# The eight modulation matrices as fp32 products instead of pairs of fp16 terms

## The reference

```
# layer 0                                        # layer 1
scale1 = cond @ ln1_tw.T                         ada = silu(cond) @ Wada.T + bada     # 64 x 3072
h = rms(x) * (ln1_w * (1 + scale1))              gamma1, gamma2, scale1, scale2, shift1, shift2 = split(ada, 6)
x = x + attention(rope(h @ Wq, h @ Wk), h @ Wv) @ Wo.T     x = x + attn(ln(x) * (scale1 + 1) + shift1) * gamma1
scale2 = cond @ ln2_tw.T                         x = x + (gelu((ln(x)*(scale2+1)+shift2) @ Wfc1.T + bfc1) @ Wfc2.T + bfc2) * gamma2
h = rms(x) * (ln2_w * (1 + scale2))
x = x + (silu(h @ Wg.T) * (h @ Wu.T)) @ Wd.T
```

## Time and profile before

| | us |
|---|---|
| median of 3 runs | 2768.59 (2766.93 to 2770.6) |
| the profiled execution, its own time | 2764.49 |
| its span, first to last instruction | 2762.7 |
| mean granted TensorE clock | 0.969 |
| TensorE busy (matmuls) | 2524.8 (91%) |
| VectorE busy | 1395.9 (51%) |
| ScalarE busy | 962.3 (35%) |
| GpSimd busy | 1040.4 (38%) |

### The profile page before, as it was taken

How to read it: one execution, slowest core, us unless ns; L and a number is a source line. 1 busy time by engine, 2 the same in 40 slices (tenths; PEclk the granted TensorE clock), 3 DMA queues, 4 the chain that set the end, 5 groups by cost and what they waited for, 6 DMA issues and landing times.

```text
span 2762.7 us, 47260 instructions
## 1 busy us (share of the span) xinstructions
PE 2524.8 (91%) x18552; PEld 1255.8 (45%) x18552; DVE 1395.9 (51%) x2115; ACT 962.3 (35%) x1549; POOL 1040.4 (38%) x1007
## 2 busy tenths in 40 slices
PE   2449999999999999999997769999999999999998
PEld 1224445454444444444443335454454545454543
DVE  4554434243342524435224657575767667575742
ACT  2332213132231322223122336262626354444532
POOL 1112223132231322223121546564655555565632
PEclk9669999999999999999999889999999999999999
DMA  6430010100001010010205111212121112112110
GB/s 201 132 98 3 7 45 3 50 3 28 26 5 48 3 46 7 12 40 4 76 3 179 36 43 29 74 31 76 28 66 44 55 42 60 48 45 65 32 54 27
DMA packets 115019, 129.40 MB, mean 47 GB/s; under 512 B 53758, under 2 KB 56190, under 8 KB 114820
## 3 DMA queue, kind: packets, MB, share of 16 engines
q1 hardware_dynamic: 114820, 126.36, 15.2%
HBM read 71.79 MB, written 18.87 MB: 33 GB/s over the span
## 4 chain that ended last, share of the span: by engine, by line
PE 73%; issue 10%; DVE 7%; POOL 5%; ACT 4%; DMA 0%; POOLq 0%; SPq 0%; DVEq 0%; ACTq 0%
PE ps_m L1440 38%; PE ps_abef L1440 18%; PE ps_d L1440 2%; PE ps_c L1440 2%; PE ps_abef L1619 2%; PE ps_abef L1621 2%; PE ps_abef L1626 2%; PE ps_abef L1653 1%; PE ps_d L1607 1%; POOL h_mlp L815 1%; POOL inner L837 1%; POOL scratch L868 1%; PE ps_abef L1642 1%; PE ps_abef L1661 1%; PE ps_c L1475 1%
## 5 line engine op out<-in xcount | busy, mean ns | idle before, releaser
L1440 PE MATMUL ps_m<-h_mlp,weights 128*128 128x512 f16 x3072 | 708.5, 383 | 38.9 <-POOL h_mlp L815 19.1
L1440 PE MATMUL ps_m<-weights,inner 128*128 128x512 f16 x3072 | 690.4, 379 | 8.7 <-DVE scratch L1280 8.7
L1440 PEld LDWEIGHTS ps_m<-h_mlp,weights 128*128 128x128 f16 x3072 | 296.8, 99 | 384.9 <-issue 38.4
L1440 PEld LDWEIGHTS ps_m<-weights,inner 128*128 128x128 f16 x3072 | 296.9, 98 | 346.1 <-DVE scratch L1280 6.5
L837 POOL TENSOR_TENSOR inner<-scratch,inner 128x512 f16<-128x512 f32 x256 | 301.0, 1176 | 315.6 <-ACT inner L1000 315.6
L1440 PE MATMUL ps_abef<-h_mlp,weights 128*128 128x512 f16 x1536 | 345.4, 379 | 0.0
L1440 PEld LDWEIGHTS ps_abef<-h_mlp,weights 128*128 128x128 f16 x1536 | 147.6, 98 | 173.0
L806 POOL TENSOR_TENSOR scratch<-scratch 128x1 f32<-128x1 f32 x128 | 29.1, 228 | 434.3 <-ACT scratch L945 379.1
L1000 ACT CAST inner<-scratch 128x512 f16<-128x512 f32 x256 | 156.6, 612 | 101.6 <-DVE scratch L1408 68.1
L815 POOL TENSOR_TENSOR h_mlp<-scratch,h_mlp 128x512 f16<-128x512 f32 x64 | 74.0, 1156 | 199.2 <-ACT h_mlp L958 199.2
L1278 DVE SCALAR_TENSOR_TENSOR scratch<-scratch,ps_m 128x512 f32<-128x512 f32 x64 | 44.0, 688 | 198.2 <-ACT scratch L1008 198.2
(11 more groups left out here) (169 smaller groups left out, 3646.3 us busy)
## 6 DMA issues: line engine op xcount, KB each, us to landing
x_mlp<-x_attn SPq DMA_DIRECT2D x64, 256.0 KB, 2.3
weights<-gamma SPq DMA_DIRECT2D x128, 128.0 KB, 2.9
scratch<-scratch SPq DMA_DIRECT2D x128, 128.0 KB, 2.6
x_attn<-x SPq DMA_DIRECT2D x32, 256.0 KB, 2.7
x_mid<-x_mlp SPq DMA_DIRECT2D x32, 256.0 KB, 2.0
x_attn<-x_mid SPq DMA_DIRECT2D x32, 256.0 KB, 2.7
out<-x_mlp SPq DMA_DIRECT2D x32, 256.0 KB, 2.2
inner<-wada_t SPq DMA_DIRECT2D x6, 1024.0 KB, 5.9
```

Source lines behind the costliest of these rows:

```text
L1440: ins = nc.tensor.matmul(o, left(a, k), right(b, k), start=(first and n == 0), stop=(last and n == len(order) - 1), skip_group_check=True)
```

## The change

The modulation matrices are no longer cut. TensorE multiplies them as fp32 straight from the staging buffer, with fp32 conditioning rows (`cond32` for matrices 0 and 1, `silu32` for the others). 16 fp32 matmuls of 64 columns take the place of 48 fp16 ones, and for matrices 2 and 3, whose product is stored the other way round, 4 of 512 columns the place of 12. The products wait for the load instead of the cut, and a load into a buffer that held a modulation matrix waits for that matrix's product (`s_ada`). Since these matrices don't count in `s_whi` and `s_wlo` any more, `cut_no(g)` gives the number of cut groups up to g. The factor 1/16 falls out of VectorE's modulation terms.

```
@@ load_group, on SP
-                if reuse >= 0:
-                    sp.wait_ge(s_wlo, reuse + 1)
+                if reuse >= 0 and groups[reuse][0] == "ada":
+                    sp.wait_ge(s_ada, ada_before(reuse) + 1)
+                elif reuse >= 0:
+                    sp.wait_ge(s_wlo, cut_no(reuse))
...
@@ ScalarE
-            nc.scalar.copy(cond_cut[:, 0], cond32).then_inc(s_setup_act, 1)
-            nc.scalar.activation(xn[:, 0:256].rearrange("p (k b) -> p k b", k=KC), cond32, ACT.Tanh, scale=0.5).then_inc(s_setup_act, 1)
+            nc.scalar.activation(silu32, cond32, ACT.Tanh, scale=0.5).then_inc(s_setup_act, 1)
...
-            cut_hi(0)
-            for g in range(1, FIRST):
+            for g in range(2, FIRST):
                 cut_hi(g)
...
-                if FIRST + s < SETUP:
+                if FIRST + s < SETUP and groups[FIRST + s][0] == "w":
                     cut_hi(FIRST + s)
...
@@ VectorE
-            link(nc.vector.tensor_tensor(cond_cut[:, 1], cond32, cond_cut[:, 0], ALU.subtract))
-            link(nc.vector.scalar_tensor_tensor(half_silu, half_silu, 1.0, cond32, ALU.add, ALU.mult))
-            link(nc.vector.tensor_scalar(half_silu, half_silu, 0.5, None, ALU.mult))
-            link(nc.vector.tensor_copy(silu_cut[:, 0], half_silu))
-            nc.vector.tensor_tensor(silu_cut[:, 1], half_silu, silu_cut[:, 0], ALU.subtract).then_inc(s_cond, 1)
+            link(nc.vector.scalar_tensor_tensor(silu32, silu32, 1.0, cond32, ALU.add, ALU.mult))
+            nc.vector.tensor_scalar(silu32, silu32, 0.5, None, ALU.mult).then_inc(s_cond, 1)
...
-            cut_lo(0)
             dve.wait_ge(s_const, 43)
...
-                if FIRST + s < SETUP:
+                if FIRST + s < SETUP and groups[FIRST + s][0] == "w":
                     cut_lo(FIRST + s)
...
@@ TensorE
             def ada(g, n):
-                pe.wait_ge(s_wlo, g + 1)
+                landed, count, _, _ = place(g)
+                pe.wait_ge(landed, count)
                 pe.wait_ge(s_cond, 1)
...
-                c = cond_cut if n < 2 else silu_cut
+                c = cond32 if n < 2 else silu32
                 if 2 <= n < 4:
-                    ins = products([(bank[0:NSEQ, :], lambda b, k: ada_cut[:, b, k, :])],
-                                   lambda a, k: c[:, a, k, :], range(KC))
+                    for k in range(KC):
+                        ins = nc.tensor.matmul(bank[0:NSEQ, :], c[:, k, :], staged(g)[:, k, :], start=(k == 0), stop=(k == KC - 1))
                 else:
                     for f in range(KC):
-                        ins = products([(bank[:, NSEQ * f:NSEQ * (f + 1)], lambda b, k: c[:, b, k, :])],
-                                       lambda a, k: ada_cut[:, a, k, P * f:P * (f + 1)], range(KC))
+                        for k in range(KC):
+                            ins = nc.tensor.matmul(bank[:, NSEQ * f:NSEQ * (f + 1)], staged(g)[:, k, P * f:P * (f + 1)],
+                                                   c[:, k, :], start=(k == 0), stop=(k == KC - 1))
                 ins.then_inc(s_ada, 1)
```

More of the change, by code:

```diff
@@ L315, in layers_kernel @@
         cond32 = carve(256).rearrange("p (k b) -> p k b", k=KC)
-        cond_cut = carve(256).bitcast(F16).rearrange("p (h k b) -> p h k b", h=2, k=KC)
-        silu_cut = carve(256).bitcast(F16).rearrange("p (h k b) -> p h k b", h=2, k=KC)
+        silu32 = carve(256).rearrange("p (k b) -> p k b", k=KC)
         taken["scratch"] = base
@@ L527, in dest, with cut_no @@
         def dest(g, hl):
-            if groups[g][0] == "ada":
-                return ada_cut[:, hl]
             return groups[g][1][:, hl]
+        def cut_no(g):
+            return sum(1 for q in groups[:g + 1] if q[0] == "w")
         def weight_scale(g):
@@ L643, in _ @@
                 load_group(g)
-            sp.wait_ge(s_setup, 17)
+            sp.wait_ge(s_setup, 14)
             sp.dma_start(rope_dram[:, :, 0, :], cos_t.rearrange("p (t f) -> p t f", f=32)).then_inc(s_rope_st, 16)
@@ L733, in _ @@
                     store_y(L0, x_mid, NBLK - 1, t)
-            sp.wait_ge(s_wlo, SWAP)
+            sp.wait_ge(s_wlo, cut_no(SWAP - 1))
             sp.wait_ge(L0.y_out, 16 * TILES * NBLK)
@@ L920, in cut_hi @@
                 act.wait_ge(s, n)
-                if groups[g][0] == "ada":
-                    act.wait_ge(s_ada, ada_before(g))
                 if SETUP <= g < SWAP:
@@ L1029, in _ @@
             nc.scalar.copy(bias_rows[0:4, :], bias_hi[0:4, :]).then_inc(s_l1k, 1)
-            act.wait_ge(s_wlo, SWAP)
+            act.wait_ge(s_wlo, cut_no(SWAP - 1))
             def attn1(stage, it, t, norms):
@@ L1133, in ada @@
                 if n < 2:
-                    link(nc.vector.tensor_scalar(ada_f32, feat, INV, 1.0, ALU.mult, ALU.add))
+                    link(nc.vector.tensor_scalar(ada_f32, feat, 1.0, None, ALU.add))
                     w = ln_w_t[:, 4 * n:4 * (n + 1)].unsqueeze(2).to_broadcast([P, KC, NSEQ])
@@ L1140, in ada @@
                     dve.wait_ge(s_setup_dma, 64 + 32)
[L1141 to L1142 removed]
+                    nc.vector.tensor_tensor(gamma_row[0:NSEQ, :], bank[0:NSEQ, :], b_ada_bc[n - 2], ALU.add).then_inc(s_ada_out, 1)
                 else:
                     b = b_ada_t[:, 4 * (n - 2):4 * (n - 1)].unsqueeze(2).to_broadcast([P, KC, NSEQ])
[L1145 removed]
+                    ins = nc.vector.tensor_tensor(ada_f32, feat, b, ALU.add)
                     if n < 6:
@@ L1167, in _ @@
             link(nc.vector.tensor_scalar(turns, turns, -PI_IN, None, ALU.max))
-            dve.wait_ge(s_setup_act, 4)
+            dve.wait_ge(s_setup_act, 3)
             link(nc.vector.tensor_scalar(sin_t, sin_t, INV, None, ALU.mult))
@@ L1172, in _ @@
             ada_of(0)
-            for g in range(1, FIRST - 1):
+            for g in range(2, FIRST - 1):
                 cut_lo(g)
@@ L1482, in attn0 @@
                 if stage == "proj":
-                    pe.wait_ge(s_wlo, 4)
+                    pe.wait_ge(s_wlo, cut_no(3))
                     normed = norm_no(NORMS0, it, "norm1", t) + 1
@@ L1532, in attn0 @@
                 if stage == "out":
-                    pe.wait_ge(s_wlo, FIRST)
+                    pe.wait_ge(s_wlo, cut_no(FIRST - 1))
                     pe.wait_ge(L0.c_hi, n + 1)
@@ L1543, in _ @@
                     setup_group(FIRST + s)
-            pe.wait_ge(s_wlo, SETUP)
+            pe.wait_ge(s_wlo, cut_no(SETUP - 1))
             def slots0(it, both):
@@ L1682, in attn1 @@
                              first=False, late=0, ready=(L1.c_lo, n + 1)).then_inc(L1.o, 1)
-            pe.wait_ge(s_wlo, SETUP + 4)
+            pe.wait_ge(s_wlo, cut_no(SETUP + 3))
             pe.wait_ge(s_l1k, 1)
@@ L1687, in _ @@
                 attn1(stage, 0, t, NORMS1F, FIRST1)
-            pe.wait_ge(s_wlo, len(groups))
+            pe.wait_ge(s_wlo, cut_no(len(groups) - 1))
             def block1(it, both):
```

8 lines of the change are left out of this document (3 added, 5 removed).

## The result

| | before | after |
|---|---|---|
| median of the runs | 2768.89 (2766.93 to 2770.6, 4 runs) | 2725.23 (2724.91 to 2726.06, 4 runs) |
| profiled execution, its span | 2764.49, 2762.7 | 2724.91, 2723.1 |
| mean granted clock | 0.969 | 0.973 |
| VectorE, ScalarE busy | 1395.9, 962.3 | 1375.5, 947.4 |

The ratio is 0.9843 (95%: 0.9826 to 0.986): 1.6% faster, near the 2730 that was forecast and inside its range.

What follows compares the result with a forecast made beforehand. The prediction saw a 207 us setup in which TensorE mostly waits, then a TensorE-bound loop; only the setup changes. Its terms summed to 38.6 us, taking the median from 2768.6 to 2730.0, with a range of 2723 to 2744.

Steps and rivals of the forecast that it cites:

- start: Setup up to the first norm: VectorE's angle chain begins 6.45 us earlier, so the gains come earlier; 9.4 us saved.
- slot 2: Setup slot with matrix 3: product hidden before GpSimd's last cut, transposes end at 63.5 instead of 70.39; 6.9 us saved.
- slot 4: Setup slot where the product starts after the scores, with 7.1 us of cover under VectorE; 5.3 us saved.
- slot 6: Setup slot where product and stage mix follow the projection, transposes ending at 100.45 instead of 106.44; 6.0 us saved.
- slot 8: Setup slot like slot 4 with less cover for the product; 5.0 us saved.
- slot 10: Setup slot said to repeat slot 6; 6.0 us saved.
- slots 11 to 23: Setup slots from 11 on, which hold no matrix, were said to keep their length; 0 us.
- What an fp32 product costs: TensorE's fp32 matrix product of 64 columns, taken at two steps each: 4.2 us a matrix at high clock, 7.7 low.
- Costs nothing: Removed small operations, the folded scale, buffer loads waiting for the product, and slots without a matrix add no time.
- rival C: Setup loads from matrix 2 to the loop become late; two coming 4 us late leave 30.6 us, 2738; chance 0.12.
- Rival B: Stationary weight loads dominate: four steps per fp32 product, 8.3 us a matrix; saving 27.2 us, time 2741; chance 0.17.
- Rival D: Products exceed their cover in slots 4 to 10, deciding from about 14 us a matrix: 12 us slower, 2781; chance 0.04.

Runs made afterwards that it cites:

- after_third: The changed kernel, unchanged, run again on the chip of a later call for comparison: 2724.52 us, ratio 0.9846 to the kernel before.
- after_again: The changed kernel, unchanged, run and profiled once more beside the kernel before on one chip: 2723.42 us, ratio 0.9843.
- twice: The changed kernel with the fp32 products of matrices 4 to 7 made twice, the same result written again: 2731.72 us, ratio 0.9871.
- start16: The changed kernel with matrices 0 and 1 cut and multiplied as fp16 again, matrices 2 to 7 staying fp32: 2733.24 us, ratio 0.9877.
- slots16: The changed kernel with matrices 2 to 7 cut and multiplied as fp16 again, matrices 0 and 1 staying fp32: 2762.5 us, ratio 0.9982.
- four: The changed kernel with the fp32 products of matrices 4 to 7 made four times: 2758.96 us, ratio 0.9977.
- halves: The changed kernel with matrices 4 to 7 multiplied 32 conditioning rows at a time, so each stationary block is loaded twice: 2744.22 us, ratio 0.9914.

## Why the prediction was right

Term by term, before's profiled execution against after's; a term is the shrinking of the distance between two successive marks (norm, L974/L970, L1145/L1136 and so on).

| term | predicted | measured | from |
|---|---|---|---|
| start | 9.4 | 9.8 | 52.63 to 42.84 |
| slot 2 | 6.9 | 6.8 | 17.76 to 10.99 |
| slot 4 | 5.3 | 5.6 | 14.07 to 8.45 |
| slot 6 | 6.0 | 6.4 | 21.98 to 15.60 |
| slot 8 | 5.0 | 5.6 | 14.67 to 9.04 |
| slot 10 | 6.0 | 7.6 | 22.58 to 15.02 |
| slots 11 to 23 | 0 | -1.0 | 63.30 to 64.33 |
| first gate product | 38.6 | 40.7 | 206.99 to 166.27 |
| the rest | 0 | -1.1 | 2555.7 to 2556.8 |

How far can one pair of traces be trusted here? Slots 4 and 8 came out the same within 0.01 us in each further trace of either kernel. The terms whose chain runs over a projection or a late output product did not: slot 2 of the changed kernel took 12.2 us in `after_third`, where the first projection lasted 5.10 us and not 3.42, and slots 11 to 23 took 63.2 in `after_again`.

**What an fp32 product costs** was the term without a row, and the value taken, two steps, was near: each product is recorded as two matmuls, and these start 0.11 us apart high and 0.21 low, where a step was put at 0.13 and 0.24. A matrix takes 3.75 us where 4.2 was said, and 7.0 (the 13.92 of two, at the start) to 7.09 low where 7.7 was. The matrices with 512 columns were said to take 3.2 high and 6.4 low. They took 3.65 high; matrix 2 took 5.9, the end of it at the high level, and 6.6 in `after_again`. The size mattered little, because `twice` shows that even 7.3 us a matrix cost 6.2 in all.

**The start** rested on VectorE's angle chain at 5.86 (5.84 measured), SP's load of matrix 2 at 28.3 (28.17) and the gains at 42.2 (42.84 at most). The 1.0 us set aside for the stores was 0.6 in this trace and nothing in the two others (41.64, 41.57). The margin to matrix 2 was as thin as the sum had it: in `after_again` the gains were there first, and the norm waited for that product. `start16` and `slots16` show that both parts, the shorter chain of matrix 2 and the earlier angle chain, were needed for it.

**Slots 2, 6 and 10**: the transposes go right behind GpSimd's last cut, as said for slot 2; for 6 and 10 the sum had the product and the mix end 0.5 behind it. **Slots 4 and 8**: the product is hidden under VectorE, as said, so the gain is the product's full wait. **Slot 10** "repeats" slot 6 was the term mis-sized, by 1.6. Of this, 0.6 stand in before's own rows: the distance was 22.6 us in slot 10 and 22.0 in slot 6, where the projection took 5.37 for 4.82 and the transposes, from L1500 to L974, 1.24 for 0.97. The timeline of before has, with the projection of slot 6 first:

```profile
89.43 4.82 PE L1440 MATMUL ps_abef<-weights,h_attn 128*128 128x512 f16 x24
...
125.85 5.37 PE L1440 MATMUL ps_abef<-weights,h_attn 128*128 128x512 f16 x24
138.79 2.74 PE L1440 MATMUL ps_m<-scratch,x_mlp 128*128 128x64 f16 x48 [7.56 <-DVE x_mlp L1120]
141.46 1.06 PE L1528 MATMUL ps_d<-scratch 128*64 128x256 f16 x8
142.45 1.03 PE L1500 MATMUL ps_c<-ident,scratch 128*128 128x128 f16 x8
```

The other 1.0 is what is faster after the change than the sum for slot 6 had it. The projection ends 9.4 us behind the mark and not 9.8; the product of 3.74 and the mix of 0.63 are over before GpSimd's last cut, where 4.2 and 1.0 would have been 0.5 behind it; and the transposes take 0.75 and not 0.95. The clock goes with it: over product, mix and transposes it is 0.52 in before (138.7 to 143.7), behind 7.56 us of waiting, and 1.00 after the change (96.1 to 102.0), where the product follows the projection at once. I had counted the waits that go, and not all that the clock gives back on the work around them.

**Costs nothing** held for the loads (rival C): no product in slots 2 to 10 was held up by a DMA. In slot 2 it was near: matrix 3, asked for at 39.57, was there just as the projection ended, and its first weight load waited 0.26 us for it. The slots without a matrix lost 1.0 in this trace: a late output product of slot 20 takes 5.26 us at clock 0.52 where it took 3.77 at 0.73. In `after_again` it takes 3.69, so this loss does not come every time. The 1.1 in the rest lie within its scatter from trace to trace (2555.0 to 2558.7).

**Rival B** had the mechanism that the runs leave likely, that the stationary words set the length, and too high a price: four steps and 8.3 us, against two and 3.75. **Rival D**'s point, about 14 us a matrix, can be held against `four`, with 14.5: by it the gains should have been used up, and the time was still 9.9 us better than before. The start had stayed whole (the norm at 41.61), and the clock stayed high in the products.

**The median** fell by 43.7, the profiled span by 39.6. The sum was made against one execution, and added the same difference to the median. But the old kernel's executions vary more, and its profiled one was short. The forecast of 2730 is 4.8 high: 1.0 by the terms (2725.9 against the profiled 2724.91: 2.1 at the gate, less 1.1 in the rest), and 4.1 by the step to the median, of which the changed kernel has 0.3. That the clock has a part in before's scatter is shown in two of its traces, for 1.2 of the 7.1 us between them; how often each pattern comes was not measured.

## What to carry to other kernels

A dearer instruction can be the cheaper way when it takes the place of a chain over other engines: here 2.6 times the TensorE time per matrix, at the same clock, bought off two cuts that stood in line before it. Work out the cover of each place, and count in full what the new instruction takes beyond it. And give a stretch of TensorE work back its faster clock when the idle time in front of it goes; a term that "repeats" another is read from its own rows.

## What the runs showed of the hardware

- An fp32 product of 128x128 stationary words and 64 columns is recorded as two matmuls; 16 products take 3.75 us at clock 1.00 and 7.09 at 0.50, 0.23 and 0.44 us each. 48 fp16 products of that shape take 2.74 at 0.50, 0.057 each: one fp32 product is 7.8 of fp16. With 512 columns it is another picture: 4 products take 3.65 us at the high level, 0.91 each, where the loop's fp16 product takes 0.230 (706.7 us for 3072): 4.0 of fp16. The Trainium skill, "FP8 and Floating Point Precision", section "TensorE Precision Notes", gives four passes for true FP32. The rows agree at 512 columns. The 3.65 us a matrix that the prediction worked out by that rule, from fp16 products at the low level, stand against 7.09 at that level. At 64 the product costs twice what four passes would, and there the columns no longer set the pace (`halves`).
- The load of such a block of stationary words is recorded at 0.19 us at the high level and 0.33 at the low one, and the engine starts a new one every 0.11 and 0.21 us, two for each fp32 product. The Trainium skill, "TensorE: Matmul & The Clock Gate", section "LDWEIGHTS (loading the stationary operand)", gives a load's time in ns as its columns divided by 1.2, which is 107 ns for 128. The rows agree at the high level (0.11) and have twice that at the low one. The prediction's estimate of 6.8 us a matrix from this figure was too high for the high level, 3.75, because it counted four loads a product and the rows have two.
- Ahead of the first projection the clock column can't be read. It says 1.00 there, while the durations are those of the low level, as in this window of before with its 48 fp16 products in 2.74 us:

```profile
12.00:16.00 4.00, 2.74 (x48) 2.58 (x48) 3.86 (x6) 0.00 (x0) 0.00 (x0) 1.00 1.05 385
```

- VectorE's and ScalarE's cuts of a matrix hardly change from trace to trace (2.28 to 2.29 and 1.90 to 1.91 us), while TensorE's same 12 products of matrix 3 take 4.17 or 5.33. Part of this kernel's scatter, and so of the difference between a sum from one trace and a median, comes from there.
